# A drain behind the last product of each edge-MLP layer, in a one-core graph message-passing kernel

## The chip, the cores and the metric

The kernel runs on one core of one Trainium2 chip. The metric is the device time of one execution in microseconds (us); lower is better. Times are medians of several runs.

## The reference, cut to what matters

There are 12500 nodes with 128 features and 200000 edges sorted by destination `dst`. Each edge has a source node, four harmonics (`edge_attr_4`) and a length (`edge_weight`). All arithmetic is float32.

```python
h   = relu(layernorm(x))                         # 12500 x 128
rbf = cut(d) * sin(d * freqs) / (d * freqs)      # 200000 x 8
a1  = silu(rbf @ fc_w1 / sqrt(8))                # 8 -> 64     layer 1
a2  = silu(a1 @ fc_w2 / 8)                       # 64 -> 64    layer 2
w00, w01, w10, w11 = split(a2 @ fc_w3 / 8, 4)    # 64 -> 128   layer 3
gs, gv = (lin1 of h)[src]                        # gather of a 128-wide row for each edge
msg = concat(w00*gs*sh0, w11*<gv,sh1>, w01*gs*sh1, w10*gv*sh0)   # 256 wide
agg = segment_sum(msg, dst) / clip(count, 1)
out = x + sc(h) + tanh(agg_s @ alpha_w) * lin2(agg)
```

## The kernel before, in words

**Stages.** A first stage normalises the nodes, applies lin1, and writes the result to a table in HBM (`lin_table`). The edge loop follows. A last stage turns the remaining sums into output rows. The change lies in the edge loop alone.

**The edge loop.** The edges are taken in groups of 768 (`GROUP`, six tiles of 128). Four groups, numbered u = 0 to 3 (`SLOTS`), make one iteration; there are 65 iterations and one shorter group at the end, 261 groups in all. Below, a "slot" is the work of one group. Every engine has its own in-order queue, written out by hand, and the queues meet only in semaphores. For slot u of iteration i:

- **GpSimd** (`gather`, L970) issues six indirect DMAs, one for each tile, which gather the rows of `lin_table` into one of four buffers `lin_g`. It waits before the first for `near_ready` of the group four earlier (its buffer is then free), before the third for `h2_done`, before the fifth for `sums_ready`.
- **TensorE** runs, in this order, `layer1(i, u+3)` (L999, two products of 192 columns), `layer2(i, u+2)` (L1008, one product of 384 columns), `layer3(i, u+1)` (L1018, three products of 256 columns), `segment_sum(i, u-1)` (L1040, the far sum, 257 columns) and `near_layer(i, u)` (L1030, six products of 257 columns on half the columns of the array). A float32 product shows in the profile as two MATMULs, each with a LDWEIGHTS of its own.
- **ScalarE** runs `silu1` (L1139, waits `h1_done`), `silu2` (L1145, waits `h2_done`), `copy_w` (L1167, waits `w_ready`), `scale_lin` (L1157, waits for the gathered rows) and `copy_near` (L1172, waits `near_ready`).
- **VectorE** runs `accumulate` (L1474, waits `sums_ready`), `products` and `columns` (L1377 to L1401, wait for the gathered rows) and `late` (L1415 to L1423, waits `w_copied`), which writes `msg`. Its `basis` waits for `h1_done` before it overwrites `rbf`.
- **SyncE** loads sources, lengths, harmonics and keys two or three iterations ahead.

In the first 25 iterations TensorE, ScalarE and VectorE also do the skip connection (`turn_rows`, `skip_layer`), and in iterations 42 to 63 the finished node blocks (`turn_early`, `apply_early`).

**How TensorE signals.** In all five of its functions the last MATMUL of the function carries the increment of the semaphore, for example

```python
for j in range(PAIRS):
    mm = pe.matmul(ps_w[:, 2 * j * P:(2 * j + 2) * P], cols[:, j, :], w3[:], start=True, stop=True)
mm.then_inc(w_ready, 1)
```

so that TensorE's queue goes on to the next function with nothing between. Each of `ps_h1`, `ps_h2`, `ps_w`, `ps_near` and `ps_sums` is a single buffer, so each function also waits until the result before it has been read (`h1_ready`, `h2_ready`, `w_copied`, `near_copied`, `agg_ready`).

Of the kernel before, what the change touches and what calls it, by code (L numbers as in the profile page):

```python
# [37 lines left out]
P = 128  # L38
# [13 lines left out]
SEG = QUAD // SEGS  # L52
UNIT = 2 * SEG
# [63 lines left out]
def at_least(eng, sem, value):  # L117

    if not isinstance(value, int) or value > 0:
        eng.wait_ge(sem, value)  # L120


def gnn_kernel(nc, x, src, dst, sh, dist, node_vec, sc_ws, sc_wv, lin1_ws, lin1_wv,
# [44 lines left out]
    with ExitStack() as top:  # L168
        def sb(name, shape, dt=F32, ctx=top):
            return ctx.enter_context(nc.sbuf_tensor(name, shape, dt))  # L170
# [4 lines left out]
        w1 = sb("w1", [P, SEGS // 2, P])  # L175
        w2 = sb("w2", [P, P])
        w3 = sb("w3", [P, 2, P])
# [26 lines left out]
        with ExitStack() as st:  # L204
# [3 lines left out]
            def sem(name):  # L208
                return st.enter_context(nc.semaphore(name))
# [424 lines left out]
        with ExitStack() as st:  # L634
            def s2(name, shape, dt=F32):
                return sb(name, shape, dt, st)
# [30 lines left out]
            rbf = s2("rbf", [P, SEG])  # L667
            h1 = s2("h1", [P, 2, UNIT])
# [17 lines left out]
            ps_h1 = st.enter_context(nc.psum_tensor("ps_h1", [P, 512], F32))  # L686
            ps_h2 = st.enter_context(nc.psum_tensor("ps_h2", [P, 512], F32))
            ps_w = st.enter_context(nc.psum_tensor("ps_w", [P, 8 * P], F32))
# [35 lines left out]
            h1_done, h1_ready, h2_done, h2_ready = sem("h1_done"), sem("h1_ready"), sem("h2_done"), sem("h2_ready")  # L724
            w_ready, w_copied, w_read = sem("w_ready"), sem("w_copied"), sem("w_read")
# [94 lines left out]
            with nc.Fori(0, passes):  # L820
                nc.sync.sem_clear(range(sems[0].num, sems[0].num + len(sems)))
                nc.all_engine_barrier()
                with nc.Block() as block:
# [167 lines left out]
                    def _(pe):  # L991
                        def layer1(i, k):
                            i, k = i + k // UNITS, k % UNITS
                            if k == 0:
                                pe.wait_ge(rbf_ready, i + 1)
                            at_least(pe, h1_ready, i * UNITS + k)
                            rows = slice(k * 4 * RBF, (k + 1) * 4 * RBF)
                            for part in range(2):
                                mm = pe.matmul(ps_h1[:, part * SEG:(part + 1) * SEG], w1[rows, 2 * k + part, :], rbf[rows, :],  # L999
                                               start=True, stop=True)  # L1000
                            mm.then_inc(h1_done, 1)

                        def layer2(i, k, first=False):
                            i, k = i + k // UNITS, k % UNITS
                            if first:
                                pe.wait_ge(h1_ready, k + 1)
                            at_least(pe, h2_ready, i * UNITS + k)
                            pe.matmul(ps_h2[:, 0:UNIT], w2[:], h1[:, k % 2, :], start=True, stop=True).then_inc(h2_done, 1)  # L1008

                        def layer3(i, u):  # L1010

                            i, u = i + u // SLOTS, u % SLOTS
                            if isinstance(i, int) and (i == ITERS or (i == 0 and u == 0)):
                                pe.wait_ge(h2_ready, i * UNITS + u + 1)
                            at_least(pe, w_copied, i * SLOTS + u)
                            cols = h2[:, u % 2, :].rearrange("p (c j) -> p j c", j=PAIRS)
                            for j in range(PAIRS):
                                mm = pe.matmul(ps_w[:, 2 * j * P:(2 * j + 2) * P], cols[:, j, :], w3[:], start=True, stop=True)  # L1018
                            mm.then_inc(w_ready, 1)

                        def near_layer(i, u):

# [46 lines left out]
                        def skip_layer(i):  # L1069
# [4 lines left out]
                            mm.then_inc(sc_done, 1)  # L1074

                        layer1(0, 0)
                        layer1(0, 1)
                        layer2(0, 0, first=True)
                        layer1(0, 2)
                        layer2(0, 1, first=True)  # L1080
                        layer3(0, 0)

                        def body(i, share=False, early=False, finish=False, last=False):

                            for u in range(SLOTS):
                                if share and u == 1:
                                    turn_rows(i)
                                if not last or u + 3 <= SLOTS:
                                    layer1(i, u + 3)
                                if not last or u + 2 <= SLOTS:  # L1090
                                    layer2(i, u + 2)
                                layer3(i, u + 1)
                                if u > 0:
                                    segment_sum(i, u - 1)
                                elif not isinstance(i, int) or i > 0:
                                    segment_sum(i - 1, SLOTS - 1)
                                near_layer(i, u)
                                if share and u == 1:
                                    skip_layer(i)
                                if finish and u == 0:  # L1100
                                    apply_early(i - 1 - EARLY0, 1)
                                if early and u == 1:
                                    turn_early(i - EARLY0, 0)
                                if early and u == 2:
                                    apply_early(i - EARLY0, 0)
                                if early and u == 3:
                                    turn_early(i - EARLY0, 1)
# [577 lines left out]
```

## Time and profile before

| what | value |
|---|---|
| time, median of 3 runs | 2211.73 us (2203.23 to 2214.47) |
| span of the profiled execution, first to last instruction | 2483.8 us |
| first gather of the edge loop starts | 68.1 us into the span |
| last gather of the edge loop starts | 2454.4 us into the span |
| busy share of the span: TensorE, VectorE, GpSimd, ScalarE | 73%, 72%, 64%, 48% |
| mean granted TensorE clock | 0.826 |

The profiled execution has no timed value of its own in the results; it has its span. That span is 272 us longer than the median of the timed runs, so the profiled execution is the slower one and shares of it are not shares of the timed runs. The busy share of an engine counts its instructions and not its waits. The granted clock is given as a share: 1.00 is the upper level of TensorE's clock (2.4 GHz), 0.50 the lower (1.2 GHz).

### The profile page before, as it was taken

The numbers are of one execution on the slowest core, as the hardware profiler recorded it, in microseconds if no ns is written. First come the engines' busy times: TensorE is split into PE (matmuls) and PEld (weight loads), VectorE is DVE, ScalarE is ACT, GpSimd is POOL, SyncE is SP. The second block draws the span as 40 slices with busy tenths as digits, with TensorE's granted clock in tenths as the row PEclk, the third lists the DMA queues.
The fourth block names the chain that finished last, engine by engine and source line by source line (L and its number), as shares of the span: only waits on it lengthen the run. The fifth ranks groups of instructions, "written<-read, shape, count | busy, mean of one in ns | idle before, by whom it ended". The sixth has DMA issues, their size and how long they took to land. (4 is left out here: it accounts for less than half of the span.)

```text
span 2483.8 us, 34021 instructions
## 1 busy us (share of the span) xinstructions
PE 1811.4 (73%) x7969; PEld 1174.2 (47%) x7969; DVE 1783.0 (72%) x4669; ACT 1199.1 (48%) x3310; POOL 1578.4 (64%) x1624
## 2 busy tenths in 40 slices
PE   6577777787777777767677767667787776877777
PEld 6344444454444444444444434444554444544544
DVE  8577767767776777767676667767677776777777
ACT  6354545455454555444444344445444444445443
POOL 7566666666666666666666666666666666666563
PEclk9588878878888887788787878888888888888889
DMA  7322222222222222222122222222222222222222
GB/s 214 70 64 67 56 64 66 66 56 66 66 59 62 67 65 56 55 48 50 46 50 48 48 48 49 54 50 64 57 67 62 59 65 66 53 64 61 59 66 55
DMA packets 347699, 155.73 MB, mean 63 GB/s; under 512 B 237983, under 2 KB 322048, under 8 KB 347584
## 3 DMA queue, kind: packets, MB, share of 16 engines
q0 software_dynamic: 50016, 102.51, 15.7%
q1 hardware_dynamic: 296938, 51.75, 11.4%
q14 instruction: 86, 0.70, 0.1%
q8 instruction: 29, 0.48, 0.1%
q10 hardware_dynamic: 630, 0.29, 0.0%
HBM read 134.27 MB, written 20.15 MB: 62 GB/s over the span
## 5 line engine op out<-in xcount | busy, mean ns | idle before, releaser
L970 POOL DMA_INDIRECT lin_g<-lin_table,src_ix x1563 | 1530.0, 979 | 865.1 <-issue 441.5
L1157 ACT ACTIVATE lin_sh<-lin_g,harm 128x128 f32<-128x128 f32 x1563 | 483.8, 396 | 94.6 <-DMA lin_g<-lin_table,src_ix 87.6
L1040 PE MATMUL ps_sums<-near_sums,far_hot 128*128 128x257 f32 x520 | 208.0, 488 | 440.8 <-DVE agg L1474 206.0
L1030 PE MATMUL ps_near<-msg,onehot 128*64 128x257 f32 x3126 | 507.5, 471 | 1.2 <-DVE msg L1423 1.2
L1018 PE MATMUL ps_w<-w,h 128*128 128x256 f32 x1566 | 462.6, 440 | 28.2 <-ACT key_all L1167 18.5
L1018 PEld LDWEIGHTS ps_w<-w,h 128*128 128x128 f32 x1566 | 395.3, 272 | 135.4 <-issue 44.9
L999 PE MATMUL ps_h<-rbf,w 32*128 32x192 f32 x1044 | 277.0, 390 | 138.0 <-issue 67.1
L1415 DVE TENSOR_TENSOR msg<-lin_sh,key_all 128x576 f32<-128x576 f32 (+1 forms) x261 | 197.3, 756 | 249.9 <-ACT key_all L1167 209.5
L1167 ACT ACTIVATE key_all<-ps_w 128x768 f32<-128x768 f32 x261 | 213.5, 818 | 305.2 <-remote 188.6
L1030 PEld LDWEIGHTS ps_near<-msg,onehot 128*64 128x64 f32 x3126 | 241.3, 164 | 230.6 <-issue 175.7
L1383 DVE TENSOR_TENSOR lin_sh<-lin_g,ps_meta 128x576 f32<-128x576 f32 (+1 forms) x261 | 196.6, 753 | 212.2 <-DMA lin_g<-lin_table,src_ix 207.0
L1040 PEld LDWEIGHTS ps_sums<-near_sums,far_hot 128*128 128x128 f32 x520 | 105.1, 230 | 503.9 <-issue 387.7
L1172 ACT ACTIVATE near_sums<-ps_near 128x257 f32<-128x257 f32 x261 | 99.4, 381 | 474.1 <-remote 342.1
L999 PEld LDWEIGHTS ps_h<-rbf,w 32*128 32x128 f32 x1044 | 189.1, 212 | 228.0 <-issue 176.2
L1008 PE MATMUL ps_h<-h,w 128*128 128x384 f32 x522 | 278.8, 620 | 0.4 <-issue 0.3
L1474 DVE SCALAR_TENSOR_TENSOR agg<-ps_sums,at_lo,agg 128x257 f32 x260 | 126.1, 485 | 190.7 <-issue 188.0
L1401 DVE TENSOR_REDUCE dot<-lin_sh 128x192 f32<-128x576 f32 (+1 forms) x261 | 210.5, 806 | 0.0
L1139 ACT ACTIVATE h<-ps_h 128x384 f32<-128x384 f32 x261 | 127.8, 490 | 141.2 <-remote 74.0
L1423 DVE TENSOR_TENSOR msg<-w_s,ps_meta 128x576 f32<-128x576 f32 (+1 forms) x261 | 195.2, 748 | 0.0
L1145 ACT ACTIVATE h<-ps_h 128x384 f32<-128x384 f32 x261 | 129.1, 494 | 82.9 <-PE ps_h L1008 40.4
L1398 DVE TENSOR_TENSOR onehot<-iota,ps_meta 128x384 f32<-128x384 f32 (+1 forms) x261 | 142.8, 547 | 0.0
L1474 DVE SCALAR_TENSOR_TENSOR agg<-ps_sums,at_hi,agg 128x257 f32 x260 | 123.8, 476 | 0.0
(175 smaller groups left out, 1655.2 us busy)
## 6 DMA issues: line engine op xcount, KB each, us to landing
lin_g<-lin_table,src_ix POOLq DMA_INDIRECT x1563
dist_in<-in_edge_weight SPq DMA_DIRECT2D x67, 96.0 KB
lin_table<-lin_out SPq DMA_DIRECT2D x24, 256.0 KB, 2.6
x_in<-in_x SPq DMA_DIRECT2D x24, 256.0 KB
skip_table<-x_in SPq DMA_DIRECT2D x24, 256.0 KB
xq<-in_x SPq DMA_DIRECT2D x23, 256.0 KB, 3.9
harm<-in_edge_attr SPq DMA_DIRECT2D x66, 48.0 KB
x_in<-skip_table SPq DMA_DIRECT2D x8, 256.0 KB
```

What stands on the lines that cost most here:

```text
L970: pool.indirect_dma_start(slot_tiles(s, u)[rows, t, :], None, lin_table, bass.IndirectOffsetOnAxis(ap=src_ix[rows, s.phase, u, col:col + 1 ...
L999: mm = pe.matmul(ps_h1[:, part * SEG:(part + 1) * SEG], w1[rows, 2 * k + part, :], rbf[rows, :], start=True, stop=True)
L1008: pe.matmul(ps_h2[:, 0:UNIT], w2[:], h1[:, k % 2, :], start=True, stop=True).then_inc(h2_done, 1)
L1018: mm = pe.matmul(ps_w[:, 2 * j * P:(2 * j + 2) * P], cols[:, j, :], w3[:], start=True, stop=True)
L1030: mm = pe.matmul(ps_near[half * NEAR:(half + 1) * NEAR, 0:MSG + 1], onehot[:, u, t, :], msg[:, u % 2, t, :], start=(j == 0), stop=(j == PA ...
L1040: pe.matmul(ps_nodes(i), far_hot[:, u, :], near_sums[:, u % 2, :], start=True, stop=True).then_inc(sums_ready, 1)
L1157: last = act.activation(lin_sh0[:, u % 2, j, :], slot_tiles(s, u)[:, j, :], ACT.Copy, scale=harm[:, s.phase, u, harm_col(j):harm_col(j) + 1])
L1167: act.activation(w_sb[:, u % 2, :], ps_w[:, 0:TILES * P], ACT.Copy).then_inc(w_copied, 1)
L1383: dve.tensor_tensor(lin_sh[:, h], lin_v(s, u)[:, h], sh_vec(u)[:, h], ALU.mult).then_inc(lin_sh_ready, 1)
L1401: dve.tensor_reduce(dot[:, u % 2, h], lin_sh[:, h].rearrange("p t m c -> p t c m"), AX_X, ALU.add).then_inc(dot_ready, 1)
L1415: dve.tensor_tensor(o10[:, h], scaled[:, h, MUL:].rearrange("p t (m c) -> p t m c", m=3), spread_m(w_part(u, 2))[:, h], ALU.mult)
L1474: dve.scalar_tensor_tensor(out=rows, in0=ps_nodes(i), scalar=part[:, bass.ds(g, 1)], in1=rows, op0=ALU.mult, op1=ALU.add).then_inc(added, 1)
```

## The change

The three layers of the edge MLP no longer put their increment on the last MATMUL. Each issues a drain on TensorE behind its last product, and the drain carries the increment. `near_layer` and `segment_sum` keep theirs on the MATMUL. There are three drains for each slot, 783 in an execution. No product, semaphore or wait is added or taken away, and the order stays.

```diff
                             for part in range(2):
-                                mm = pe.matmul(ps_h1[:, part * SEG:(part + 1) * SEG], w1[rows, 2 * k + part, :], rbf[rows, :],
+                                pe.matmul(ps_h1[:, part * SEG:(part + 1) * SEG], w1[rows, 2 * k + part, :], rbf[rows, :],
                                                start=True, stop=True)
-                            mm.then_inc(h1_done, 1)
+                            pe.drain(fusable=False).then_inc(h1_done, 1)
 ...
-                            pe.matmul(ps_h2[:, 0:UNIT], w2[:], h1[:, k % 2, :], start=True, stop=True).then_inc(h2_done, 1)
+                            pe.matmul(ps_h2[:, 0:UNIT], w2[:], h1[:, k % 2, :], start=True, stop=True)
+                            pe.drain(fusable=False).then_inc(h2_done, 1)
 ...
                             for j in range(PAIRS):
-                                mm = pe.matmul(ps_w[:, 2 * j * P:(2 * j + 2) * P], cols[:, j, :], w3[:], start=True, stop=True)
-                            mm.then_inc(w_ready, 1)
+                                pe.matmul(ps_w[:, 2 * j * P:(2 * j + 2) * P], cols[:, j, :], w3[:], start=True, stop=True)
+                            pe.drain(fusable=False).then_inc(w_ready, 1)
```

## Rows read from the trace of the kernel before

**Rows 1.** The page: span, and busy time of each engine.

```profile
span 2483.8 us, 34021 instructions
PE 1811.4 (73%) x7969; PEld 1174.2 (47%) x7969; DVE 1783.0 (72%) x4669; ACT 1199.1 (48%) x3310; POOL 1578.4 (64%) x1624
```

**Rows 2.** Groups by line, GpSimd's gathers: busy, mean ns of one, idle before.

```profile
L970 POOL DMA_INDIRECT lin_g<-lin_table,src_ix x1563 | 1530.0, 979 | 865.1 <-issue 441.5 <-remote 325.1 <-PE ps_sums L1040 41.7
```

**Rows 3.** Timeline of GpSimd: a steady pair of gathers, and the last one.

```profile
1207.33 0.94 POOL L970 DMA_INDIRECT lin_g<-lin_table,src_ix  x1 [0.30 <-issue]
1208.58 0.94 POOL L970 DMA_INDIRECT lin_g<-lin_table,src_ix  x1 [0.30 <-issue]
...
2454.36 0.92 POOL L970 DMA_INDIRECT lin_g<-lin_table,src_ix  x1 [1.82 <-PE ps_h L1008]
```

**Rows 4.** Two stretches, TensorE slot at each clock level: busy (instructions), clock, DMA.

```profile
1203.68:1208.55 4.87, 4.87 (x27) 3.39 (x26) 3.27 (x9) 3.54 (x11) 3.68 (x4) 1.00 0.20 53
1229.34:1240.24 10.90, 8.83 (x27) 5.30 (x26) 7.25 (x18) 2.36 (x6) 5.83 (x7) 0.53 0.14 36
```

**Rows 5.** Timeline of TensorE at clock 1.00: products, then weight loads.

```profile
1205.14 0.91 PE L999 MATMUL ps_h<-rbf,w 32*128 32x192 f32 x4
1205.98 0.91 PE L1008 MATMUL ps_h<-h,w 128*128 128x384 f32 x2
1206.73 1.46 PE L1018 MATMUL ps_w<-w,h 128*128 128x256 f32 x6
...
1205.98 0.30 PEld L1008 LDWEIGHTS ps_h<-h,w 128*128 128x128 f32 x2 [0.23 <-issue]
1206.41 1.44 PEld L1018 LDWEIGHTS ps_w<-w,h 128*128 128x128 f32 x6
1207.81 0.41 PEld L1040 LDWEIGHTS ps_sums<-near_sums,far_hot 128*128 128x128 f32 x2
```

**Rows 6.** Timeline of TensorE at clock 0.50: products, then weight loads.

```profile
1217.94 2.84 PE L1030 MATMUL ps_near<-msg,onehot 128*64 128x257 f32 x12
...
1220.71 1.64 PE L999 MATMUL ps_h<-rbf,w 32*128 32x192 f32 x4
...
1233.68 1.64 PE L999 MATMUL ps_h<-rbf,w 32*128 32x192 f32 x4 [2.07 <-DVE rbf L1367]
1235.25 1.65 PE L1008 MATMUL ps_h<-h,w 128*128 128x384 f32 x2
1236.69 2.77 PE L1018 MATMUL ps_w<-w,h 128*128 128x256 f32 x6
...
1236.05 0.34 PEld L1018 LDWEIGHTS ps_w<-w,h 128*128 128x128 f32 x1 [0.30 <-issue]
...
1238.83 0.76 PEld L1040 LDWEIGHTS ps_sums<-near_sums,far_hot 128*128 128x128 f32 x2
1240.24 0.85 PEld L1030 LDWEIGHTS ps_near<-msg,onehot 128*64 128x64 f32 x10 [0.66 <-issue]
```

**Rows 7.** Who waited for whom, whole kernel: us in total, times, longest.

```profile
ACT near_sums L1172 <- remote: 342.1, 81, 6.4
POOL lin_g L970 <- remote: 325.1, 155, 3.2
DVE msg L1415 <- ACT key_all L1167: 209.5, 113, 4.4
ACT key_all L1167 <- remote: 188.6, 46, 10.4
```

**Rows 8.** Timeline of TensorE, ScalarE and GpSimd around one long wait.

```profile
1208.55 1.52 PE L1030 MATMUL ps_near<-msg,onehot 128*64 128x257 f32 x12
...
1211.60 1.46 PE L1018 MATMUL ps_w<-w,h 128*128 128x256 f32 x6
...
1216.35 0.39 ACT L1172 ACTIVATE near_sums<-ps_near 128x257 f32<-128x257 f32 x1 [5.39 <-remote]
...
1216.78 1.23 PE L1040 MATMUL ps_sums<-near_sums,far_hot 128*128 128x257 f32 x2 [3.73 <-ACT near_sums L1172]
...
1217.06 0.94 POOL L970 DMA_INDIRECT lin_g<-lin_table,src_ix  x1 [2.25 <-remote]
```

## The prediction

> **What bounds the kernel now.** I read the page's busy times first. No engine is full: TensorE has 73% of the span, VectorE 72%, GpSimd 64% [rows 1]. The chain that ended last covers only the last eleven microseconds, so it says nothing of the loop. I therefore went to the groups by line and the waits.
>
> GpSimd is what paces the loop. A gather that waits for nothing takes 0.94 us and follows the one before by 1.25 us (1207.33 to 1208.58) [rows 3], so six of them need 7.5 us. From the first gather, 68.1 us into the span, to the last, at 2454.36 [rows 3], there are 2386 us for 261 slots. The idle time before the 1563 gathers is 865 us [rows 2]; 0.30 us before each is the ordinary gap of [rows 3], which makes 469 us, so about 396 us are true waits. Without them the loop would take 2386 - 396 = 1990 us, 7.62 us for each slot. Around the loop lie 68 us ahead and 2483.8 - 2454.4 = 29 us behind, 98 us together.
>
> The timed runs have a median of 2211.7 us, 272 us under the profiled span. If the parts around the loop are equal in both, the loop takes 2211.7 - 98 = 2114 us there, 8.10 us for each slot, and only 2114 - 1990 = 124 us are waits of GpSimd. This is the room that the change can play with downwards: nothing that TensorE does can bring the time under 1990 + 98 = 2088 us.
>
> TensorE's pace depends on its clock. At granted clock 1.00 a slot takes 4.87 us, and TensorE is busy for all of it [rows 4]: far below 7.62 us, so TensorE waits for messages, not the other way round. At clock 0.50 the parts of a slot are, from start to start, layer 1 1.57, layer 2 0.80, layer 3 2.78, far sum 1.41 and near products 2.77 us [rows 6], 9.33 us together (the far sum's is the gap from 1238.83 to 1240.24, near products' from 1217.94 to 1220.71). That is above 7.62. So TensorE sets the pace where its clock is low, GpSimd where it is high. If all 124 us came from such slots, at 9.33 - 7.62 = 1.71 us each, there would be 73 of them in 261.
>
> There is one more thing to see. ScalarE's copy of the near sums waits 342 us for a "remote" releaser and GpSimd 325 us [rows 7]. In one such case the near products end at 1210.07, layer 3 ends at 1213.06 and TensorE then stands idle; yet the copy starts at 1216.35, and the far sum behind it at 1216.78 [rows 8]. So TensorE's signals reach the others up to 6 us after the modelled end of the MATMUL that carries them. Since the profiled execution is 272 us slower than the timed ones and these waits are of that order, I take most of the lateness to belong to the profiled execution.
>
> **The change part by part.** The increments of `h1_done`, `h2_done` and `w_ready` move from a MATMUL to a drain. Nothing is computed or waited for differently, and nothing of SyncE's or GpSimd's is moved. The cost is that TensorE's next function can no longer begin while the last MATMUL runs. Queued behind each drain are: behind layer 1's, the load and products of layer 2; behind layer 2's, layer 3; behind layer 3's, the far sum and behind it the near products, for which GpSimd waits.
>
> At clock 1.00, layer 1's products end at 1205.14 + 0.91 = 1206.05, and layer 2's load starts at 1205.98: an overlap of 0.07. Layer 2 ends at 1206.89, layer 3's load starts at 1206.41: 0.48. Layer 3 ends at 1208.19, the far sum's load starts at 1207.81: 0.38 [rows 5]. Together 0.93 us of overlap are lost for each slot. At clock 0.50 the same three are 1235.32 - 1235.25 = 0.07, 1236.90 - 1236.05 = 0.85 and 1239.46 - 1238.83 = 0.63, together 1.55 us [rows 6].
>
> On top comes the drain itself and the start of the instruction behind it. No drain of this kind is in the trace. From below, the far sum starts 0.04 us after the end of the copy it waits for (1216.35 + 0.39 = 1216.74, 1216.78 [rows 8]). From above, the gap of 0.30 us that stands before a load of layer 3 with "issue" as its reason [rows 6]. I take 0.10, nearer to the first, since a drain has no operand to fetch. Three of them are 0.3 us (0.1 to 0.9).
>
> So a slot of TensorE becomes 4.87 + 0.93 + 0.3 = 6.1 us at the high clock (up to 6.7), still under 7.62. What hides this is GpSimd's issue of the gathers; if GpSimd took under 6.1 us the whole 1.2 us would show. At the low clock it becomes 9.33 + 1.55 + 0.3 = 11.2 us, and 1.85 us more for each slot is on the path.
>
> If all 73 such slots pay in full, that is 135 us. Not all do: GpSimd has three further groups to issue before it needs a slot's near products, so it rides out part of a delay. In [rows 8] TensorE stood still for 3.73 us and GpSimd for 2.25 us, a share of 0.6, which makes 81 us. The other end is 0, if the buffers cover it. I take 45 us, a little over the middle, because the low-clock spells come in runs that use up what the buffers cover. ScalarE and VectorE get the results of layer 3 later by the delays of all three drains, and VectorE already waits 209 us for that copy [rows 7]; this is the same path, not a second cost.
>
> The sum: 2211.7 + 45 = 2257 us.
>
> The page "PSUM — Partial Sum Buffer" of the Trainium skill, section "Engine vs sequencer instructions", asks to put the increment on the matmul itself, and says that a drain waits until the engine is fully idle. By that rule the overlaps that [rows 5, 6] show are lost whole, as the sum has them, and a drain brings no earlier signal.
>
> **The rivals.** *Hidden.* Low-clock slots are fewer than 73 in the timed runs, and the 124 us come from gathers that land late or from the extra node work; then TensorE's 6.1 us lie beside 7.62 us of gathers. For it speaks that even with drains TensorE has 1.5 us to spare in a high-clock slot; against it that the mean granted clock of the profiled execution is 0.826, which puts TensorE at 0.50 for about a third of it. Time 2212, within 11 us.
>
> *The drains cure late signals* (the other side). If the lateness of [rows 7, 8] is in the timed runs too, and it is tied to an increment that travels with a MATMUL or to TensorE running ahead, then a drain, which is done only when the products are, stops TensorE from piling up unfinished signals, and layers 2 and 3 reach ScalarE on time. The place is ScalarE's wait at L1139, L1145 and L1167 and what stands behind it. The price is at most the 124 us of waits, less the drains' own 45; if it gets back 105 of them the time is 2211.7 - 105 + 45 = 2152. It decides from 45 us of recovered waits on. Against it: near products and far sums keep their increments, and those are the ones that GpSimd waits for most, and the room of 124 us is small beside the 396 us of the profiled run, so most of the lateness seems not to be there when timed.
>
> The page "NOTIFIC — the notification-queue block" of the Trainium skill, section "Overflow: three behaviours, one of which stalls the engine", says that profile records are written through a path that can hold an engine up. It would make the lateness the profiler's alone; the trace agrees in so far as the profiled execution is the longer one.
>
> *The clock stays low.* The three pauses make TensorE's stream thinner. At the low clock a slot with drains takes 11.2 us, 3.6 us above the gathers' pace, so every further tenth of the slots (26) that runs at 0.50 costs 94 us. With one tenth more the time is 2257 + 94 = 2351. For it: the stretch at 0.53 already had TensorE idle for 2 us of 10.9 [rows 4]. Against it: a TensorE that is the bound is busier, and that is where the clock was granted in full.
>
> **How the numbers follow.** The forecast has 0.45, hidden 0.22, late signals cured 0.20, clock 0.13. I call a difference under 0.5%, 11 us, none that this measurement can tell. A little of the forecast's case and of the cure's ends within it, and a little of the hidden case on the far side, which leaves faster 0.21, same 0.22, slower 0.57. The forecast's own range goes from 2223 (nearly all absorbed) to 2318 (81 us, and the drain at 0.30 instead of 0.10, which is 0.6 us more in 73 slots at a share of 0.6: 81 + 26 = 107). The range reaches down to the cure's 2152, taken as 2150, and up towards the clock's 2351, taken as 2335; about 0.1 is left out on either side.
>
> **What the profile of the changed kernel would show.** The loads of layers 2 and 3 and of the far sum start behind the end of the products before them, by 0.05 to 0.30 us, where they overlapped by 0.07, 0.48 and 0.38. A full TensorE slot at clock 1.00 takes about 6.1 us, not 4.87. The gathers in the high-clock stretches still follow each other by 1.25 us. If the cure is right, ScalarE's "remote" waits at L1167 and L1139 nearly vanish and its wait at L1172 shrinks with them. If the clock rival is right, the mean granted clock falls clearly below 0.82. The prediction is wrong if the drain itself costs much more than 0.30 us, or if the lateness of TensorE's signals is as large in the timed runs as in the profiled one and hangs on who carries the increment.

## The result and the profile after

The kernel with the drains is slower: 2288.5 us (median of 4 runs, 2277.8 to 2295.6) against 2211.6 us of the kernel before, a ratio of 1.0346 (95% interval 1.031 to 1.0383), +77 us. I had forecast 2257 and a range of 2150 to 2335: the direction is right, the size is not.

One thing must be said before the traces are compared. The profiled execution of [rows 1 to 8], 2483.8 us, is not like any other of that kernel: profiled again in the first experiment it took 2204.9 us, in line with its timed runs. From here on, "before" in a trace means that second profile.

The page of the kernel after: span, busy times, and the group of the gathers (busy, mean ns of one, idle before).

```profile
span 2293.9 us, 34804 instructions
PE 1788.0 (78%) x7969; PEld 1076.9 (47%) x7969; DVE 1777.8 (78%) x4669; ACT 1238.1 (54%) x3310; POOL 1575.5 (69%) x1624
...
L970 POOL DMA_INDIRECT lin_g<-lin_table,src_ix x1563 | 1527.2, 977 | 675.5 <-issue 420.0
```

The page of the kernel before, profiled again.

```profile
span 2204.9 us, 34021 instructions
PE 1710.7 (78%) x7969; PEld 1137.6 (52%) x7969; DVE 1776.8 (81%) x4669; ACT 1235.6 (56%) x3310; POOL 1581.6 (72%) x1624
...
L970 POOL DMA_INDIRECT lin_g<-lin_table,src_ix x1563 | 1532.7, 981 | 582.3 <-issue 428.4
```

The work is the same: VectorE, ScalarE and GpSimd are busy for the same microseconds, within 7. What grows is idle time. With the ordinary gap of 0.30 us before each of the 1563 gathers (469 us) taken off, GpSimd truly waits 582.3 - 469 = 113 us before and 675.5 - 469 = 207 us after. Its pace without these waits is the one of the prediction: the timeline of GpSimd after has the first gather at 68.67, the last at 2262.30.

```profile
68.67 1.12 POOL L970 DMA_INDIRECT lin_g<-lin_table,src_ix  x1 [8.06 <-issue]
...
1172.51 0.94 POOL L970 DMA_INDIRECT lin_g<-lin_table,src_ix  x1 [1.64 <-PEq L1009]
1173.76 0.94 POOL L970 DMA_INDIRECT lin_g<-lin_table,src_ix  x1 [0.30 <-issue]
1176.92 1.11 POOL L970 DMA_INDIRECT lin_g<-lin_table,src_ix  x1 [2.22 <-PE ps_sums L1041]
1178.34 0.94 POOL L970 DMA_INDIRECT lin_g<-lin_table,src_ix  x1 [0.31 <-issue]
1179.59 0.94 POOL L970 DMA_INDIRECT lin_g<-lin_table,src_ix  x1 [0.30 <-PEq L1009]
...
2262.30 0.92 POOL L970 DMA_INDIRECT lin_g<-lin_table,src_ix  x1 [1.19 <-PEq L1009]
```

2262.30 - 68.67 = 2193.6 us, less 207 of waits is 1987 us; the prediction had 1990. The rows also show where the waits are: two long ones close together (for layer 2, then for the far sum), then gathers at the ordinary pitch of 1.25 us as in [rows 3]. That pattern returns once in an iteration. Summed over the kernel without its first four groups, and with 0.30 us taken off before each gather, the waits of an iteration's first group of gathers grow from 45 to 141 us; the fourth group has 56 before and 53 after, the other two 2 to 3 us.

TensorE's slot at clock 1.00, the answer to [rows 4] and [rows 5]: the window (length, busy and instructions of TensorE, its loads, VectorE, ScalarE, GpSimd, then clock, DMA share, GB/s), and the timeline of its products and loads.

```profile
1209.28:1215.17 5.89, 5.50 (x28) 3.27 (x26) 4.37 (x11) 3.81 (x12) 4.37 (x6) 1.00 0.17 45
```

```profile
1209.29 0.91 PE L999 MATMUL ps_h<-rbf,w 32*128 32x192 f32 x4
1210.28 0.91 PE L1008 MATMUL ps_h<-h,w 128*128 128x384 f32 x2
1211.27 1.62 PE L1019 MATMUL ps_w<-w,h 128*128 128x256 f32 x6
...
1210.27 0.30 PEld L1008 LDWEIGHTS ps_h<-h,w 128*128 128x128 f32 x2 [0.37 <-issue]
1211.26 1.29 PEld L1019 LDWEIGHTS ps_w<-w,h 128*128 128x128 f32 x6 [0.69 <-issue]
1213.09 0.30 PEld L1041 LDWEIGHTS ps_sums<-near_sums,far_hot 128*128 128x128 f32 x2 [0.54 <-issue]
1213.72 1.07 PEld L1031 LDWEIGHTS ps_near<-msg,onehot 128*64 128x64 f32 x12 [0.33 <-issue]
```

The three overlaps are gone. Layer 1 ends at 1209.29 + 0.91 = 1210.20 and layer 2's load starts at 1210.27; layer 2 ends at 1211.19, the next load starts at 1211.26; layer 3 ends at 1212.89, the far sum's load starts at 1213.09. So a drain and the start behind it take 0.07, 0.07 and 0.20 us. The slot is 5.89 us, against 4.87 in [rows 4] and the 6.1 forecast. Counted from load to load, layer 1 to 2 grew by 0.15 us, 2 to 3 by 0.56, 3 to the far sum by 0.43, and the far sum to the near products shrank by 0.11.

Who waits for whom, in answer to [rows 7] (us in total, times, longest): first the kernel before, profiled again.

```profile
DVE lin_sh L1383 <- DMA lin_g<-lin_table,src_ix: 112.8, 122, 2.4
DVE msg L1415 <- ACT key_all L1167: 64.8, 79, 4.0
...
POOL lin_g L970 <- PE ps_sums L1040: 82.7, 81, 7.0
POOL lin_g L970 <- PE ps_h L1008: 53.9, 73, 7.1
...
ACT near_sums L1172 <- PE ps_near L1030: 240.7, 73, 10.7
```

Then the kernel after.

```profile
DVE msg L1416 <- ACT key_all L1168: 152.3, 75, 4.5
DVE lin_sh L1384 <- DMA lin_g<-lin_table,src_ix: 110.3, 122, 2.1
...
POOL lin_g L970 <- PE ps_sums L1041: 147.1, 98, 7.5
POOL lin_g L970 <- PEq L1009: 102.5, 126, 8.5
```

No "remote" releaser is left in either. The row to look at is the first of after: VectorE waits 152.3 us, not 64.8, for ScalarE's copy of layer 3, and in no more places (75 against 79). That is 87.5 of the 89 us between the two spans. It is again one place in an iteration: counted by group, 149.9 of the 152.3 us stand at the messages of group u = 2, once in each of the 65 iterations (before, 54.7 of the 64.8 us, in 59 of them). Here is one of them in the timeline of after, from VectorE's basis to VectorE's messages:

```profile
1201.44 0.35 DVE L1368 TENSOR_TENSOR rbf<-frac,ps_meta 128x192 f32<-128x192 f32 x1
...
1201.93 0.91 PE L999 MATMUL ps_h<-rbf,w 32*128 32x192 f32 x4 [1.42 <-DVE rbf L1368]
...
1202.90 0.49 ACT L1140 ACTIVATE h<-ps_h 128x384 f32<-128x384 f32 x1 [1.70 <-PEq L1001]
...
1202.92 1.07 PE L1008 MATMUL ps_h<-h,w 128*128 128x384 f32 x2
...
1204.06 0.49 ACT L1146 ACTIVATE h<-ps_h 128x384 f32<-128x384 f32 x1 [0.67 <-PEq L1009]
...
1204.08 2.92 PE L1019 MATMUL ps_w<-w,h 128*128 128x256 f32 x6
...
1207.06 0.81 ACT L1168 ACTIVATE key_all<-ps_w 128x768 f32<-128x768 f32 x1 [2.52 <-PEq L1020]
...
1207.90 0.76 DVE L1416 TENSOR_TENSOR msg<-lin_sh,key_all 128x576 f32<-128x576 f32 x1 [1.88 <-ACT key_all L1168]
```

VectorE makes the basis of the next iteration. Layer 1 of the next iteration waits for it, and since TensorE's queue is in order, layer 2 of this iteration's last group and layer 3 of the one before stand behind it, although neither needs that basis. ScalarE's copy waits for layer 3, and VectorE, which has some 3.1 us of other work meanwhile, waits for the copy. In the other slots TensorE runs ahead; here the three layers run one behind the other on the path, with VectorE at both ends. I call this the chain.

Its length can be read in each of 64 iterations as a window from the end of the basis to the end of the copy. Two of these windows and their sum, before:

```profile
168.93:172.96 4.03, 3.89 (x18) 2.97 (x20) 3.15 (x9) 2.72 (x7) 2.95 (x4) 1.00 0.17 49
...
1106.85:1113.61 6.76, 6.63 (x16) 4.40 (x17) 3.17 (x8) 1.79 (x4) 4.71 (x5) 0.50 0.17 49
...
sum 302.66, PE 296.64 PEld 216.78 DVE 197.29 ACT 140.55 POOL 201.99; mean PE 4.63 PEld 3.39 DVE 3.08 ACT 2.20 POOL 3.16
```

And after:

```profile
1168.24:1175.61 7.37, 6.84 (x14) 3.98 (x14) 3.17 (x8) 1.79 (x4) 3.90 (x5) 0.50 0.16 44
...
1572.84:1577.37 4.53, 4.08 (x16) 2.54 (x16) 3.14 (x9) 2.02 (x5) 2.44 (x3) 1.00 0.29 43
...
sum 399.93, PE 368.07 PEld 212.58 DVE 201.23 ACT 119.71 POOL 232.42; mean PE 5.75 PEld 3.32 DVE 3.14 ACT 1.87 POOL 3.63
```

The 64 chains take 302.7 us before and 399.9 after, while VectorE's work in them stays at 197 and 201: its idle time there grows from 105 to 199 us. At equal clock a chain grows by only 0.50 us at the high level (4.03 to 4.53) and 0.61 at the low one (6.76 to 7.37), 32 to 39 us for 64. The rest, some 60 us, is the clock: 34 of the 64 chains ran wholly at the high level before, 13 after; 5 before and 23 after had a granted clock of 0.55 or less. Weighted by time, the granted clock in the chains fell from 0.84 to 0.67, while the mean over the whole span rose from 0.860 to 0.888.

### The profile page after: what moved, and what is told of

Its sections match the earlier page's. It is cut to its first block and busy times, and to the rows that moved or that the text cites. A ratio compares the mean times of both kernels' runs of the same rounds, so it can differ in the third digit from the quotient of the medians.

```text
span 2293.9 us, 34804 instructions
## 1 busy us (share of the span) xinstructions
PE 1788.0 (78%) x7969; PEld 1076.9 (47%) x7969; DVE 1777.8 (78%) x4669; ACT 1238.1 (54%) x3310; POOL 1575.5 (69%) x1624
## 5 line engine op out<-in xcount | busy, mean ns | idle before, releaser
L970 POOL DMA_INDIRECT lin_g<-lin_table,src_ix x1563 | 1527.2, 977 | 675.5 <-issue 420.0
L1019 PE MATMUL ps_w<-w,h 128*128 128x256 f32 x1566 | 482.7, 451 | 26.6 <-issue 8.8
L1019 PEld LDWEIGHTS ps_w<-w,h 128*128 128x128 f32 x1566 | 362.9, 266 | 225.4 <-issue 208.5
L1031 PE MATMUL ps_near<-msg,onehot 128*64 128x257 f32 x3126 | 436.9, 418 | 0.1
L1041 PE MATMUL ps_sums<-near_sums,far_hot 128*128 128x257 f32 x520 | 194.4, 458 | 308.3 <-DVE agg L1475 273.1
L999 PE MATMUL ps_h<-rbf,w 32*128 32x192 f32 x1044 | 258.4, 370 | 118.6 <-DVE rbf L1368 117.8
L1416 DVE TENSOR_TENSOR msg<-lin_sh,key_all 128x576 f32<-128x576 f32 (+1 forms) x261 | 196.5, 753 | 163.0 <-ACT key_all L1168 152.3
L1031 PEld LDWEIGHTS ps_near<-msg,onehot 128*64 128x64 f32 x3126 | 215.8, 146 | 189.7 <-issue 121.2
L1008 PE MATMUL ps_h<-h,w 128*128 128x384 f32 x522 | 268.2, 599 | 26.8 <-issue 9.3
L1041 PEld LDWEIGHTS ps_sums<-near_sums,far_hot 128*128 128x128 f32 x520 | 85.1, 206 | 404.2 <-issue 402.8
L999 PEld LDWEIGHTS ps_h<-rbf,w 32*128 32x128 f32 x1044 | 174.6, 197 | 195.7 <-issue 154.9
L1008 PEld LDWEIGHTS ps_h<-h,w 128*128 128x128 f32 x522 | 85.3, 206 | 109.6 <-issue 109.6
```

The source lines that it names most:

```text
L970: pool.indirect_dma_start(slot_tiles(s, u)[rows, t, :], None, lin_table, bass.IndirectOffsetOnAxis(ap=src_ix[rows, s.phase, u, col:col + 1 ...
L1031: mm = pe.matmul(ps_near[half * NEAR:(half + 1) * NEAR, 0:MSG + 1], onehot[:, u, t, :], msg[:, u % 2, t, :], start=(j == 0), stop=(j == PA ...
L1041: pe.matmul(ps_nodes(i), far_hot[:, u, :], near_sums[:, u % 2, :], start=True, stop=True).then_inc(sums_ready, 1)
L1416: dve.tensor_tensor(o10[:, h], scaled[:, h, MUL:].rearrange("p t (m c) -> p t m c", m=3), spread_m(w_part(u, 2))[:, h], ALU.mult)
```

## The experiments

Line numbers move by some lines with each edit; the operations are the same. "Cost" below is the ratio to the kernel before times its median, in the same call.

**Is it the kernel, or its first profile?** e1 is the kernel before, unchanged.

> The kernel before, unchanged. All theories: time 2205 to 2218 us. What it decides is the profiled execution. If the late TensorE signals (ScalarE's remote waits of 342 us at L1172, GpSimd's of 325 us) belong to that one profiled execution, this trace has few of them and a span near 2210 us; if recording always causes them in this kernel, the span is again near 2480 us while the timed runs stay at 2211 us; if they are in the timed runs too, the span and the time of the profiled execution are near 2211 us with the remote waits still there.

2205.2 us, ratio 0.9996 (0.9981 to 1.001), profiled at 2204.9 with a granted clock of 0.860. The profile is shown above: no "remote" waits, and TensorE's signals reach the others some 14 to 25 ns behind the modelled end of their MATMUL; 2 of 1305 were over 1 us late, against more than half in the trace of [rows 1 to 8]. The count of that trace is rough, since it has only 1095 semaphore updates for 1305 signals. The lateness of [rows 7, 8] belonged to that one execution.

**The signal or the pause?** e2 leaves the increments on the products and puts the three drains behind them all the same. No one waits for a drain; only the engine's order feels it.

```
-    pe.drain(fusable=False).then_inc(h1_done, 1)
+    mm.then_inc(h1_done, 1)
+    pe.drain(fusable=False)
     ... (the same for h2_done and w_ready)
```

> All three drains are issued, but the increments stay on the last MATMUL of each layer. Theory A (the pause: TensorE's next function can no longer overlap the last product) expects the whole cost, 2275 to 2300 us. Theory B (the signal: ScalarE and VectorE get each layer's result later because a drain fires later than the MATMUL) expects most of the cost gone, 2211 to 2240 us. The rival that drains deliver signals more promptly expects this one slower than the changed kernel, above 2300 us.

2288.5 us, 1.0386 (1.0353 to 1.0419). That is all of the loss (1.0346 with the signals on the drain; the intervals meet at 1.035 to 1.038). Who carries the increment doesn't matter. What costs is the pause: TensorE may not begin the next layer.

**One drain alone.** e3 has only layer 1's, e4 only layer 3's.

```
e3:  layer 1 by a drain, layers 2 and 3 signal at the product
e4:  layer 3 by a drain, layers 1 and 2 signal at the product
```

> Only layer 1 signals by a drain. Theory A: the cost follows the overlap lost, 0.17 of 1.2 us in a slot at the high clock, so about a seventh of the 77 us: 2222 us (2215 to 2230). A fixed price for each drain, wherever it stands, expects a third: 2237 us.

> Only layer 3 signals by a drain. Theory A: 0.4 to 0.5 of 1.2 us, about 0.4 of the 77 us: 2242 us (2232 to 2252). A fixed price for each drain expects 2237 us, not to be told from it here; that layer 3's result is what VectorE waits for, so that its drain carries nearly all of the cost, expects 2270 us or more.

e3 2230.0 us, 1.0108 (1.0077 to 1.0138), +24 us; e4 2230.5, 1.0115 (1.0087 to 1.0144), +25 us. e3 is at the upper edge of what its expectation had for a cost by lost overlap, e4 below it. Layer 1's drain takes 0.15 us from a slot of TensorE, layer 3's 0.32 (0.43 less the 0.11 given back), and both cost the same. The time does not follow what a drain takes from TensorE's slots. The chains show what it does follow. At the high level a chain takes 4.10 us in e3 and 3.97 in e4, against 4.03 before: layer 3's drain doesn't lengthen it at all. Yet the 64 chains take 347 us in each of the two, against 303 before, because only 19 of them (e3) and 8 (e4) ran wholly at the high level, against 34. Layer 2's drain alone was not run; if the three costs add up, some 28 us are left to it.

**Which slots pay?** The prediction let any slot at the low clock pay. e5 has the three drains only in the part of the loop body with u equal to 1, where layer 1 waits for the basis, one slot in four; e6 has them in the other three parts.

```
+    def last_of(mm, by_drain):
+        return pe.drain(fusable=False) if by_drain else mm
...
-    pe.drain(fusable=False).then_inc(h1_done, 1)
+    last_of(mm, by_drain).then_inc(h1_done, 1)
...
-    layer1(i, u + 3)
+    layer1(i, u + 3, by_drain=u == 1)     # e6: u != 1; layers 2, 3 alike
```

> The three drains stand only in TensorE's part u = 1 of each iteration (one slot in four), where layer 1 of the next iteration waits for VectorE's basis and layers 2 and 3 and a far sum, for which GpSimd waits, are queued behind it. Theory C (the cost is the latency of that one chain, once for each iteration) expects nearly the whole cost: 2265 to 2290 us. Theory A as predicted (low-clock slots of any number pay alike) expects a quarter of it: 2220 to 2232 us.

> The drains stand in u = 0, 2 and 3 and not in u = 1. Theory C expects 2205 to 2222 us. Theory A expects three quarters of the cost: 2255 to 2270 us.

e5 2270.3 us, 1.0277 (1.0259 to 1.0294), +61 us. e6 2227.6 us, 1.0075 (1.0057 to 1.0093), +17 us. Together 78, the whole change. A quarter of the drains makes nearly four fifths of the cost. The other three quarters cost 17 us, some 6 us more than the top of what I had expected. e6 has no drain in the chain, and at the high level its chains are as short as before (3.96 us); but only 15 of the 64 ran wholly at that level, and together they take 342 us. So drains outside the chain reach the time through the clock inside it.

**Take the layers out of the chain.** e7 (without drains) and e8 (with) issue layer 1 of the next iteration behind this part's layers 2 and 3 and its far sum, so that only layer 1 stands behind the basis on TensorE. ScalarE's order stays.

```
     for u in range(SLOTS):
-        if not last or u + 3 <= SLOTS:
+        if u != 1 and (not last or u + 3 <= SLOTS):
             layer1(i, u + 3)
+        if u == 1:
+            pe.wait_ge(h1_ready, i * UNITS + u + 3)
         ... layer2(i, u + 2), layer3(i, u + 1), segment_sum ...
+        if u == 1 and (not last or u + 3 <= SLOTS):
+            layer1(i, u + 3)
         near_layer(i, u)
```

> The kernel before, with layer 1 of part u = 1 moved behind layer 2, layer 3 and the far sum of that part, so that these no longer queue behind the wait for the basis. Theory C expects GpSimd's waits before the first group of an iteration (55 us in the kernel before) to shrink to 15 us or less and the time to 2160 to 2190 us, unless the near products, now right behind layer 1, become what is late. If that chain is not the bound, 2205 to 2220 us.

> The same move in the changed kernel, with its drains. Theory C expects most of the drains' cost to vanish, since they no longer lie between the basis and GpSimd's waits: 2170 to 2210 us, against 2288 without the move. If the cost of the drains is TensorE's throughput in every slot, they still cost 60 us or more over the kernel with the move and without drains.

e7 2190.3 us, 0.9908 (0.989 to 0.9926), 20 us faster than before, at the edge of what I had expected; e8 2212.9 us, 1.0014 (0.9997 to 1.0031), 3 us above the range expected. The same three drains that cost 77 us cost 23 here. In e7's timeline the layers lie beside VectorE's basis, not behind it:

```profile
1121.49 0.91 PE L1008 MATMUL ps_h<-h,w 128*128 128x384 f32 x2
...
1122.24 1.46 PE L1018 MATMUL ps_w<-w,h 128*128 128x256 f32 x6
...
1124.07 0.35 DVE L1373 TENSOR_TENSOR rbf<-frac,ps_meta 128x192 f32<-128x192 f32 x1
1126.03 0.67 PE L1040 MATMUL ps_sums<-near_sums,far_hot 128*128 128x257 f32 x2 [2.33 <-DVE agg L1480]
...
1126.63 0.91 PE L999 MATMUL ps_h<-rbf,w 32*128 32x192 f32 x4
...
1127.58 0.49 ACT L1145 ACTIVATE h<-ps_h 128x384 f32<-128x384 f32 x1 [5.34 <-PE ps_h L999]
1127.97 0.48 ACT L1151 ACTIVATE h<-ps_h 128x384 f32<-128x384 f32 x1
1128.34 0.82 ACT L1173 ACTIVATE key_all<-ps_w 128x768 f32<-128x768 f32 x1
...
1129.19 0.76 DVE L1421 TENSOR_TENSOR msg<-lin_sh,key_all 128x576 f32<-128x576 f32 x1 [0.54 <-ACT key_all L1173]
```

Layer 3 is done at 1123.70, before the basis; a drain behind it can only take from the 2.33 us for which TensorE then stands idle. It also shows why the gain is small: the copy could start at 1123.7, but ScalarE has the activation of layer 1 ahead of it in its queue and waits for that until 1127.58. VectorE's waits say the same: e7's gain is in its wait for the gathers (112.8 to 78.5 us), while its wait for the copy grew (64.8 to 81.8). ScalarE's order moved as well would be the next step; it was not tried.

**More drain.** e9 has two drains behind each layer, the second of which carries the increment.

```
+    pe.drain(fusable=False)
     pe.drain(fusable=False).then_inc(h1_done, 1)
     ... (the same for h2_done and w_ready)
```

> The changed kernel with two drains behind each layer instead of one, the second with the increment. It prices the drain itself, apart from the overlap that the first one already takes. If a drain costs about 0.05 us, as the load behind it in the changed kernel's trace suggests, three more on the chain of each of the 65 iterations cost 10 us: 2290 to 2303 us. If it costs 0.3 us, the upper bound of the prediction, 58 us or more: above 2340 us.

2320.5 us, 1.0494 (1.0469 to 1.052): 32 us on top of the single drains. In the trace a second drain adds 0.077 us. Three in each of 65 chains are 15 us, and the profiled executions differ by as much (2308.6 against 2293.9 us); the timed medians differ by twice that. The agreement proves little: at the high level a chain did grow from 4.53 to 4.77 us, but the 64 chains together grew only from 399.9 to 402.3 us, because fewer of them ran at the low level (14 against 23), and the runs of either kernel lie 13 to 18 us apart. Where the 32 us stand is open. Neither of the two ranges expected was hit.

**Are GpSimd's waits the way in?** e10 (without drains) and e11 (with) leave GpSimd only the wait for the near products; its waits for layer 2 ahead of a group's third gather and for the far sum ahead of its fifth are taken away.

```
-    if not first and k == 2:
-        pool.wait_ge(h2_done, s.i * SLOTS + u)
-        pool.nop(nofuse=True)
-    if not first and k == 4:
-        pool.wait_ge(sums_ready, s.i * SLOTS + u - SLOTS + 1)
-        pool.nop(nofuse=True)
```

> The kernel before, in which GpSimd waits only for near_ready (its buffer is free) and no longer for h2_done before the third and sums_ready before the fifth gather. Theory C (nearly all of GpSimd's waits are these two, and the buffers have slack beyond them) expects 2100 to 2160 us. If the wait merely moves to near_ready, or the gathers that now run ahead slow others down, 2190 to 2230 us.

> The same in the changed kernel. Theory C expects the drains to cost at most 25 us over the kernel of the run before, since TensorE's latency behind the basis no longer holds GpSimd. If their cost is TensorE's throughput, it stays at 60 us or more.

e10 2179.0 us, 0.9853 (0.9827 to 0.988), 33 us faster than before and the fastest of all, though between the two ranges expected. e11 2268.8 us, 1.0237 (1.02 to 1.0273): the drains cost 90 us between the two, where at most 25 had been expected if GpSimd's two waits were the place. So they are not. The expectation gave 60 us or more to TensorE's throughput; e5, e6 and e8 speak against that, and it had not thought of VectorE. The rows of VectorE's waits, e10:

```profile
DVE msg L1409 <- ACT key_all L1161: 90.4, 77, 3.7
DVE lin_sh L1377 <- DMA lin_g<-lin_table,src_ix: 59.3, 83, 2.5
```

and e11:

```profile
DVE msg L1410 <- ACT key_all L1162: 207.5, 107, 5.0
DVE lin_sh L1378 <- DMA lin_g<-lin_table,src_ix: 29.3, 43, 1.8
```

The gathers now come early enough (29.3 us of waits for them), and the whole cost of the drains stands at the copy: 154 of the 207.5 us at group u = 2, most of the rest at the group behind it. GpSimd's one wait that is left, for the near products, grows from 93 to 177 us between the two. The near products come behind VectorE's messages, so I read GpSimd's longer waits in the kernel after as a consequence of VectorE's, not as their cause. e10 also confirms GpSimd's pace once more: e10's gathers run from 67.94 to 2144.85 with 559.3 us idle, 2076.9 - (559.3 - 469) = 1987 us.

**Both cures together.** e12 has e7's order and e10's single wait, no drains.

```
e7's edit of TensorE's body and e10's edit of the gathers
```

> No drains, layer 1 of part u = 1 behind the far sum, and GpSimd waiting only for near_ready: both remedies together. If the two remove the same wait, as theory C says, it is within 15 us of the better of the two alone.

2192.8 us, 0.9905 (0.9878 to 0.9931), within 15 us of the better one as expected: the two gains don't add, and with e7's order nothing of e10's is left. VectorE's two waits are 78.8 and 80.2 us: what the copy gives, the gathers' order does not use. Why was not followed further.

**All in one table.** us of the profiled execution, VectorE's two waits as in the rows above, and what is left of the span.

```
run                        drains   span   copy_w  gathers  span less both
e1  before                 no      2204.9    64.8   112.8   2027.3
after                      yes     2293.9   152.3   110.3   2031.3
e2  pause only             yes     2283.6   141.8   111.0   2030.8
e3  layer 1 only           1       2232.4    90.5   114.4   2027.5
e4  layer 3 only           1       2232.5    80.7   125.7   2026.1
e5  drains at u = 1        yes     2265.5   123.9   117.2   2024.4
e6  drains elsewhere       yes     2227.8    83.6   117.7   2026.5
e7  late layer 1           no      2188.4    81.8    78.5   2028.1
e8  late layer 1           yes     2212.7    94.9    90.9   2026.9
e9  two drains             2 each  2308.6   169.3   109.9   2029.4
e10 near wait only         no      2175.6    90.4    59.3   2025.9
e11 near wait only         yes     2269.3   207.5    29.3   2032.5
e12 e7 and e10             no      2193.3    78.8    80.2   2034.3
```

The last column is the same within 10 us for all 13, although the spans lie 133 us apart. So two rows of the waits of one engine account for the differences here to within 10 us. VectorE is busy for 1775 to 1779 us in all of them. It is idle in a third place as well, before `accumulate`, for 188 to 193 us in every one; that wait doesn't change with the drains and is part of the last column. The sum alone doesn't single VectorE out: GpSimd's idle time beyond the 469 us of ordinary gaps, taken off the spans, leaves 2085 to 2102 us for the same 13. The two engines wait in step. What puts the entry at VectorE is e11 and the place of the wait, at the end of the chain.

## Why the prediction was right in direction and short in size

**GpSimd's pace: confirmed, but it was half of the picture.** Floor 1990 us forecast, 1987 measured in two kernels; true waits of 124 us forecast for the timed runs, 113 measured. I took from it that GpSimd paces the loop. But no run comes near that floor (the nearest is e10, 91 us above the 2088), and VectorE's wait at the end of the chain is where the cost enters. GpSimd and VectorE hold each other in a ring; I had only looked at one of them.

**The drain and the lost overlap: right.** 0.10 us for each forecast, 0.07 to 0.20 measured; a slot of 6.1 us forecast at the high clock, 5.89 measured; the gathers in such stretches keep their 1.25 us.

**The step that failed** is "If all 73 such slots pay in full, that is 135 us. Not all do: GpSimd has three further groups to issue before it needs a slot's near products", with the sentence on VectorE behind it, "this is the same path, not a second cost". The cost is not spread over the slots at low clock, to be cut down by what GpSimd rides out. e5 and e6 put 61 of 78 us on one slot in four; e11 shows that it enters at VectorE's wait for ScalarE's copy even when GpSimd's two waits are gone. The share of 0.6 by which the 135 us were cut was itself read from [rows 8], a stall with a late signal, of the kind that only that disturbed execution has. VectorE's wait for the copy stood in [rows 7] with 209 us, most of it from the same disturbance (65 us in e1), and in [rows 6] layer 1 waits 2.07 us for VectorE's basis: had I followed that second row on to the copy I would have found the chain. Priced there, 0.93 + 0.3 us less what lies behind layer 3 is 0.75 us at the high clock (the loss behind layers 1 and 2, with their drains) and some 1.1 at the low one; in 65 chains that is 49 to 73 us. The trace has 0.50 and 0.61 for it, 32 to 39 us. That my middle value, 81 us, lay nearer to the 77 than the 45 I took is chance: it priced other slots.

**What neither estimate had** is the clock at that place. In the chains the granted clock went from 0.84 to 0.67, and this makes the larger part of the 97 us by which they grew, some 60 us. Not all that a chain loses reaches the time: in e6 the chains grew by 39 us and the time by 17. The rival *The clock stays low* had the right mechanism and the wrong measure: it looked for a mean below 0.82, and the mean rose to 0.888. What a stall costs is set by the clock where the path runs through TensorE, not by its mean.

Why the clock is low just there is only partly shown. e3, e4 and e6 show that pauses outside the chain, or ones that hardly lengthen it, bring it down too. In the 5 us ahead of a chain TensorE is busy for 3.85 us before, and for 3.54 after, 3.47 in e2, 3.52 in e5 and 3.60 in e6. e10, without any drain, has 3.58 there, and its chains run at 0.75. So a TensorE that idled a little more ahead of the chain goes with a lower clock in it. The clock falls inside the chain rather than before: it stood at the low level at the start of 15 chains before and of 21 after, but halfway through 21 before and 46 after. No experiment changed the idle time alone, so this link is argued, not shown.

**The two other rivals.** *The drains cure late signals* had no object. The late signals belonged to one execution, as e1 shows, and e2 shows that the carrier of the signal makes no difference. The 272 us between that profile and the timed runs were the hint; the prediction read it so and still gave the rival 0.20. *Hidden* was nearly true of three slots in four (e6, +17 us) and wrong for the fourth.

## What to carry to other kernels

Before you price a stall on an engine that is "only" 78% busy, look for the place in an iteration where its queue stands behind another engine's result and that engine in turn waits for what lies further back in the queue; here a stall there cost 61 us for a quarter of the drains, and 17 us for the other three quarters. Sum the long waits of each engine over several versions, and break the one that moves down by its place in the iteration; more than one engine can pass the test of the sum, and an experiment that takes away a wait (e11) tells which comes first. The order of functions in a queue matters too: e7's order gains 20 us and cuts the cost of the same drains from 77 to 23. And don't set a completion signal on a drain where the last product can carry it: nothing is signalled earlier, and the next layer's load loses its place beside this layer's products.

## What the runs showed of the hardware

The mean granted clock and the time can rise together: 0.860 and 2204.9 us before, 0.888 and 2293.9 after, 0.899 and 2308.6 with two drains. A longer kernel with the same products is not one with a lower clock; only the clock in the windows on the path says something.

A drain of TensorE costs 0.07 us until the next load behind layers 1 and 2, 0.20 behind layer 3 where another function follows, and a second drain 0.077 us more. The Trainium skill, page "PSUM — Partial Sum Buffer", section "Engine vs sequencer instructions", says that a drain waits until the engine is fully idle; the trace agrees, the drain is over some 0.02 us behind the modelled end of the last MATMUL and never before it.

TensorE's completion signals come within some 25 ns of the modelled end of the product, in the execution where I measured it (e1, all but 2 of 1305); in the one of [rows 1 to 8], as far as its incomplete records tell, more than half came over 1 us late, and the span was 13% longer. The other twelve profiled executions have no "remote" waits either. What disturbed that execution is not known.
